# First expert layer of a two-layer mixture-of-experts network on one core: upward products a tile ahead of the downward ones, and two buffers for the result rows

## What is computed

```python
xf = _ln_t(t).reshape(-1, 256)                 # 4096 tokens
probs = softmax(xf @ gate_w.T)                 # 8 experts
vals, idx = top_k(probs, 2)
w = vals / (vals.sum(-1, keepdims=True) + 1e-08)
h = einsum('nd,ehd->neh', xf, w1)              # 512 hidden
g = einsum('nd,ehd->neh', xf, w3)
eo = einsum('neh,edh->ned', silu(h) * g, w2)
t = t + einsum('ned,ne->nd', eo, comb)         # comb holds w at idx
```

## Time and profile before

| what | value |
|---|---|
| device time, median of 3 runs | 1194.84 us (1193.18 to 1196.61) |
| profiled execution | 1198.09 us |
| its span in the profile | 1196.3 us |
| busy share of the span | PE 75%, DVE 64%, ACT 51%, POOL 43% |
| first expert layer, start of tile 0 on PE to start of tile 34 | 316.39 to 627.04 us |
| DMA engines' busy share, tiles 4 to 33 | 0.86 |
| granted TensorE clock, tiles 4 to 33 | 1.00 of full speed |

### The profile page before, as it was taken

The page is one execution under the profiler, slowest core; times in us unless marked ns, Lnnn a source line. Parts: engine busy times, 40 slices in busy tenths (PEclk is TensorE's granted clock), DMA queues, the critical chain, the costliest instruction groups (busy, mean ns, idle before and its releaser), DMA issues.

```text
span 1196.3 us, 25602 instructions
## 1 busy us (share of the span) xinstructions
PE 892.9 (75%) x7009; PEld 723.3 (60%) x7009; DVE 765.6 (64%) x1916; ACT 613.6 (51%) x1345; POOL 508.7 (43%) x408
## 2 busy tenths in 40 slices
PE   5320286855589999999994751579999999999975
PEld 4200165741367777777773640168888888888863
DVE  5899788999455555655653788835555555555540
ACT  4447286857365565565662245835434444444433
POOL 1288000000256666666663230045556555555540
PEclk8655598975699999999997875579999999999996
DMA  8249274990378888888887533255666465664438
GB/s 256 71 141 316 70 252 153 295 295 1 80 185 207 200 203 207 205 202 211 202 204 216 190 115 102 79 111 118 126 117 141 76 144 114 120 136 75 75 62 281
DMA packets 208566, 190.01 MB, mean 159 GB/s; under 512 B 98752, under 2 KB 184200, under 8 KB 208392
## 3 DMA queue, kind: packets, MB, share of 16 engines
q1 hardware_dynamic: 148344, 108.48, 32.2%
q0 software_dynamic: 27440, 38.97, 18.9%
q10 hardware_dynamic: 32736, 42.02, 11.4%
HBM read 111.22 MB, written 58.79 MB: 142 GB/s over the span
## 4 chain that ended last, share of the span: by engine, by line
PE 36%; DVE 19%; issue 15%; DMA 14%; ACTq 7%; ACT 7%; SPq 1%; DVEq 1%; POOL 0%; POOLq 0%
PE bank L796 15%; PE bank L774 13%; DMA wreg<-in_L_ffn_w_dram 5%; DMA rows_y<-region 4%; PE bank L838 2%; ACTq L313 2%; DVE region L1194 2%; DVE xt L1215 2%; ACT region L1065 2%; ACTq L1033 2%; ACT region L1069 2%; DVE region L1192 1%; PE bank L682 1%; DVE region L1583 1%; ACTq L314 1%
## 5 line engine op out<-in xcount | busy, mean ns | idle before, releaser
L774 PE MATMUL bank<-xt,wreg 128*128 x3360 | 385.1, 275 | 28.4 <-DMA xt<-region 25.7
L774 PEld LDWEIGHTS bank<-xt,wreg 128*128 128x128 f16 x3360 | 327.8, 99 | 79.9 <-issue 38.2
L542 POOL DMA_INDIRECT rows_y<-region x140 | 249.3, 1781 | 179.8 <-ACT region L1091 92.4
L796 PE MATMUL bank<-wreg,region 128*128 128x256 f16 x2520 | 294.5, 273 | 22.9 <-ACT region L1069 16.6
L796 PEld LDWEIGHTS bank<-wreg,region 128*128 128x128 f16 x2520 | 234.6, 98 | 77.5 <-ACT region L1069 30.6
L492 POOL DMA_INDIRECT region<-rows_x,region x148 | 151.6, 1024 | 270.6 <-DVE region L1492 153.5
L1074 ACT ACTIVATE region<-bank,b_t,wreg 128x256 f32<-128x256 f32 x280 | 136.0, 560 | 21.2 <-PE bank L774 20.2
L1091 ACT ACTIVATE region<-region 128x256 f32<-128x256 f32 x70 | 31.7, 500 | 193.6 <-DVE region L1598 183.0
L1065 ACT ACTIVATE region<-bank,fac 128x256 f32<-128x256 f32 x140 | 58.3, 465 | 97.7 <-PE bank L774 55.2
L1593 DVE SCALAR_TENSOR_TENSOR region<-region,wreg 128x512 f16<-128x512 f32 x140 | 105.1, 751 | 5.0
L1590 DVE TENSOR_SCALAR region<-region,wreg 128x512 f16<-128x512 f32 x140 | 70.0, 500 | 51.8 <-ACT region L1074 51.7
(11 more groups left out here) (273 smaller groups left out, 1120.3 us busy)
## 6 DMA issues: line engine op xcount, KB each, us to landing
wreg<-in_L_ffn_w_dram SPq DMA_DIRECT2D x80, 512.0 KB, 5.9
wreg<-in_L_ffn_w_dram ACTq DMA_DIRECT2D x72, 256.0 KB
split_v<-wreg ACTq DMA_DIRECT2D x36, 512.0 KB
wreg<-split_v SPq DMA_DIRECT2D x32, 512.0 KB
rows_x<-region SPq DMA_DIRECT2D x16, 512.0 KB, 5.1
rows_y<-tok SPq DMA_DIRECT2D x16, 512.0 KB, 6.1
tok<-rows_y SPq DMA_DIRECT2D x16, 512.0 KB, 6.0
wreg<-in_x_dram SPq DMA_DIRECT2D x4, 1024.0 KB, 9.5
```

What stands on the lines that cost most here:

```text
L542: nc.gpsimd.indirect_dma_start(rows_y[f], bass.IndirectOffsetOnAxis(ap=now[:, b, g_, 1:2], axis=0), y_rows[:, g_, :], None, compute_op=ALU ...
L774: last = pe.matmul(to, block, x_cols[:, bass.ds(b, 1), :, xs_, k, :].rearrange("p j r n -> p (j r) n"), start=(k == 0 and ws_ + xs_ == 0), ...
L796: last = pe.matmul(yb[:, r * C:(r + 1) * C], lhs[:, c, r * P:(r + 1) * P], block, start=first, stop=end, skip_group_check=True)
```

## The change

Only the first expert layer's order changes, and the places that depend on it.

- PE makes the upward products of tile n and then the downward products of tile n - 1 (`down0`). Ahead of tile 1 there is one set of downward products on unset data; after the loop there is one more set, of the last tile. The downward products' weights are addressed by a register (`of`, the expert of the tile in front). `up` waits for `hid_ready` of the tile in front before it writes a bank again.
- ACT does four SiLU, then the result of the tile in front (`result_of_last`), then the four copies of `hid`, then the piece as before. After the loop it copies the last result.
- DVE makes all four products and then the four subtractions. The products wait for the subtractions of the tile in front (`lo_ready`).
- The result rows have two buffers (`y_pair`), each with its own semaphore (`y_put`). POOL waits for the result one tile later: `y_copied` counts two more. It also waits, at the start of a tile, for the put of two tiles ago.
- `factors_y` has four buffers. Initial counts (`LAG`) let the first tile pass.

```diff
+        LAG = 4
+        y_pair = region[:, 1024:2048].rearrange("p (j g c) -> p j g c", j=2, g=2)
-        factors_y = region[:, 7880:7884].rearrange("p (j g) -> p j g", j=2)
+        factors_y = region[:, 7880:7888].rearrange("p (j g) -> p j g", j=4)
...
                     for g_ in range(2):
                         nc.gpsimd.indirect_dma_start(rows_y[f], bass.IndirectOffsetOnAxis(ap=now[:, b, g_, 1:2], axis=0),
-                                                     y_rows[:, g_, :], None, compute_op=ALU.add).then_inc(y_free[f], 16)
+                                                     (y_pair[:, b], y_rows)[f][:, g_, :], None, compute_op=ALU.add
+                                                     ).then_inc((y_put[b], y_free)[f], 16)
...
                         for r in range(2):
                             pool.wait_ge(xr_loaded[r][f], 16 * t + 48)
+                        if f == 0:
+                            pool.wait_ge(y_put[b], 32 * p + 16)
                         copy_lists(t, b)
...
-                        after(t, lambda m: pool.wait_ge(y_copied[f], m + 1))
+                        after(t, lambda m: pool.wait_ge(y_copied[f], m + 1 + later))
                         put(b)
...
-            def up(f, e, h, b):
-
-                ws = (w1_s, w3_s) if f == 0 else (v_s,)
+            def up(f, e, h, n):
+
+                ws, b = (w1_s, w3_s) if f == 0 else (v_s,), n % 2
                 for c in (2 * h, 2 * h + 1):
+                    if f == 0:
+                        pe.wait_ge(hid_ready, LAG * n + c + 1)
...
+            def down0(w2_of, tile):
+
+                pe.wait_ge(y_copied[0], tile + 1)
+                for c in range(4):
+                    pe.wait_ge(hi_ready[0], LAG * tile + c + 1)
+                    for hs in range(2):
+                        if hs == 1:
+                            pe.wait_ge(lo_ready[0], LAG * tile + c + 1)
...
-                            up(f, e, h, n % 2)
-
-                        for h in range(halves):
-                            down(f, e, n, h, halves)
+                            up(f, e, h, n)
+
+                        if f == 0:
+                            of = e - 1 + (n - edges[e] + 63) // 64 if e else e
+                            down0(lambda c, s_: w2_s[:, of, c, s_, :] if e == 0 else
+                                  w2_s[:, bass.ds(of, 1), c, s_, :].rearrange("p a n -> p (a n)"), n)
...
+                if f == 0:
+                    with pe.Fori(edges[E], edges[E] + 1) as n:
+                        down0(lambda c, s_: w2_s[:, E - 1, c, s_, :], n)
...
+            def result_of_last(n):
+
+                act.wait_ge(y_ready[0], n + 1)
+                before = n * 63 // 64
+                act.wait_ge(y_put[0], 32 * (before // 2) + 16)
+                act.wait_ge(y_put[1], 32 * (before * 63 // 64 // 2) + 16)
+                for g_ in range(2):
+                    last = act.activation(y_pair[:, bass.ds((n + 1) % 2, 1), g_, :].rearrange("p a c -> p (a c)"), yb[:, g_ * C:(g_ + 1) * C], ACT.Copy,
+                                          scale=factors_y[:, bass.ds((n + 3) % 4, 1), g_:g_ + 1].rearrange("p a b -> p (a b)"))
+                last.then_inc(y_copied[0], 1)
...
-                                for c in (2 * h, 2 * h + 1):
-                                    act.wait_ge(hid_ready, 2 * halves * n + c + 1)
-                                    act.activation(hid_hi[:, c], hid[:, h, (c % 2) * TILE:(c % 2 + 1) * TILE], ACT.Copy
-                                                   ).then_inc(hi_ready[f], 1)
...
                         if f == 0:
+                            result_of_last(n)
+                            for c in range(4):
+                                act.wait_ge(hid_ready, LAG * n + LAG + c + 1)
+                                act.activation(hid_hi[:, c], hid[:, c // 2, (c % 2) * TILE:(c % 2 + 1) * TILE], ACT.Copy
+                                               ).then_inc(hi_ready[f], 1)
                             split_hi(n)
...
+            with act.Fori(edges[E], edges[E] + 1) as m:
+                act.wait_ge(factors_y_ready, m)
+                result_of_last(m)
...
-                                    dve.wait_ge(silu_done[f], 2 * halves * n + c + 1)
+                                    dve.wait_ge(silu_done[f], LAG * n + c + 1)
+                                    dve.wait_ge(lo_ready[f], LAG * n + c + 1)
...
+                            for c in range(4):
+                                dve.wait_ge(hi_ready[f], LAG * n + LAG + c + 1)
+                                dve.tensor_tensor(hid_lo[:, c], half(hid[:, c // 2], c), hid_hi[:, c], ALU.subtract
+                                                  ).then_inc(lo_ready[f], 1)
```

More of the change, by code:

```diff
@@ L777, in up @@
                         last.then_inc(z_ready[f], 1)
-            def down(f, e, tile, h, halves):
+            def down0(w2_of, tile):
[5 more added lines that the diff above has]
+                            pe.wait_ge(lo_ready[0], LAG * tile + c + 1)
+                        lhs = (hid_hi, hid_lo)[hs][:, c]
+                        for r, ws_ in ((0, 0), (0, 1), (1, 0), (1, 1)) if hs == 0 else ((0, 0), (1, 0)):
+                            last = pe.matmul(yb[:, r * C:(r + 1) * C], lhs[:, r * P:(r + 1) * P], w2_of(c, ws_),
+                                             start=(c == 0 and r == 0 and hs + ws_ == 0), stop=(c == 3 and hs == 1),
+                                             skip_group_check=True)
+                last.then_inc(y_ready[0], 1)
```

82 lines of the change are left out of this document (44 added, 38 removed).

## The result

The changed kernel takes 1230.95 us (median of 4 runs, 1223.73 to 1238.87), the kernel before 1195.72 (4 runs): ratio 1.0297, 95% interval 1.0240 to 1.0353. It is slower by 35 us, where 1190.3 was forecast and 1206 was the top of the range. The profiled execution took 1236.06 us, its span is 1234.3.

A forecast was written before the change was run, and what follows sets the result against it. Links per tile were PE 8.3, ACT 8.4, POOL 8.4, fetch 8.5 us; 8.7 was taken against 8.99. Gains of 8.7 and 1.2 less 5.4 for the drain gave 4.5 us won, hence 1190.3 us, range 1178 to 1206.

The forecast's parts named there:

- The fetch link: POOL fetches tile n+3 only behind the put of tile n-1, now later; taken as the highest link, 8.5 us a tile.
- 3T = 15.2 + D: T is the tile time, 15.2 us from upward products to fetch, D from fetch through transposes; three tiles close the loop.
- its rival: Fetches and transposes slowed beside ACT's pieces: D 12.1 to 12.7, T 9.1 to 9.3, total 1202.3 to 1208 us; chance 0.22.
- I take 10.3: Choice for D, in us, between 9.1 measured with little DMA load and 18 at most; gives T = 8.5.
- the 15.2: Us from upward products' start to fetch: PE 8.2, result copies 0.9, on to the put 0.9, put to fetch 5.0.
- Queues in turn: DMA engines serve queues with work a packet at a time, so overlap with pieces doubles fetch and transpose time.
- A late piece should hold ACT less often: On ACT, the result copy between a piece's load and split lengthens first SiLU to split from 4.04 to 4.5 us.
- the surplus: Time per tile above the highest link, from links taking turns and single stalls: 0.46 us before, 0.25 taken after.
- the rivals at 8.9: ACT stays the bound with its surplus, T = 8.9: total 1196.3 us, up to 1199; chance 0.16.
- PE's turn: PE's own time per tile from upward and downward products: 8.2 to 8.6 us, taken 8.3.
- Drain: After the last tile, its put starts 16.6 us after the tile instead of 11.2: 5.4 us lost.
- 86% load: The DMA engines' busy share in the loop before, cited in favour of the slower fetch link case.

The follow-up runs named there:

- run 4: The changed kernel with each of ACT's two piece loads cut to 64 of 512 columns, stores whole: 1182.69 us, 0.9878 of the kernel before.
- run 3: The changed kernel with 12 filler matmuls per tile behind the downward products, into an unused bank: 1228.68 us, 1.0260 of the kernel before.
- run 6: The changed kernel with ACT's piece DMAs issued behind its four SiLU, after a wait for the piece under way: 1206.77 us, 1.0105 of the kernel before.
- Run 2: The changed kernel with POOL fetching the first layer's rows one tile further ahead (t+4 instead of t+3): 1217.54 us, 1.0181 of the kernel before.
- run 14: The changed kernel with piece DMAs issued by SP behind its transposes, rows fetched a tile further ahead, start mended: 1158.79 us, 0.9697 of the kernel before.
- run 13: The changed kernel with the three piece DMAs issued by SP behind its two transposes, and the start mended: 1219.63 us, 1.0171 of the kernel before.
- 15: The kernel before with the three piece DMAs issued by SP behind its transposes: 1184.26 us, 0.9901 of the kernel before.
- 5: The changed kernel with rows fetched a tile further ahead and ACT's piece DMAs behind its four SiLU, with a wait: 1205.64 us, 1.0097.
- 9: The changed kernel with rows fetched a tile further ahead, first count earlier, and ACT's piece DMAs ahead of the split, with a wait: 1237.75 us, 1.0373.
- 12: The kernel before with ACT's three piece DMAs, and a wait, between the two halves of a tile: 1291.61 us, 1.0800 of the kernel before.

## Why the prediction was wrong

**The fetch link.** 3T = 15.2 + D was the right equation, and its rival was the right mechanism, with too small a chance (0.22) and too small a price (1202 to 1208). The failed step is "I take 10.3" for D: it measured 12.9 in the mean of ten turns. I took it from fetches that land a microsecond later under load, and the earlier trace rows for the transposes, although no row showed them issued beside ACT's pieces. The fetches were about right (3.57 us); from the first fetch to the second transpose's issue it is 5.2 us, against 5.4 at the first tile of the kernel before; all the growth is in the landing of the transposes, 7.2 us for 3.4. With D = 12.9 and the 15.2 the tile would be 9.4. The rest, to 10.0, is in the 15.2, which measured 17.1: PE, held for 2.8 to 5.0 us, runs its next upward products at the lower clock in eight turns of ten, 1.5 us more in the mean, a feedback that the sum lacked, and 0.4 us is left. The runs bear out the two sizes: with small loads (run 4) the link is 15.5 + 9.9, close to what I had forecast. What mending the clock alone would give isn't shown (run 3).

**Queues in turn.** The rule quoted from the Trainium skill (DMA: Bandwidth & Descriptors, Queues, rings and completion order), that the engines serve queues with work in turn, stood in the prediction with its consequence that an overlap doubles the transposes' time. The runs agree with the doubling, though none shows the packets' turns: 3.6 us apart from the pieces (run 6), 7.2 beside them, 4.7 beside the whole store and an eighth of the loads (run 4). I gave it too little weight.

**ACT and the pieces.** "A late piece should hold ACT less often" failed: late pieces hold it 17.9 us in the loop, where it was 3.3. Run 2 takes the fetch link away and has 9.52 us, not 8.4 to 8.7, as the same meeting makes a piece land in 6.4 us instead of 4.2. So the surplus and the rivals at 8.9 were beside the point; the real second bound was not among them.

**PE and fill.** PE's turn, taken as 8.2 to 8.6, is 7.88: 5.24 us from upward to downward products and 2.64 on to the next tile, where I had 5.32 from a tile of the old order and 2.90 from its first. Tiles 0 to 3 won 3.0 us, where I forecast 1.2 and nothing for the fill. The start's 1.8 us was missed: I costed the initial counts at nothing and didn't look at what DVE does before it gives them.

**Drain.** Forecast 5.4 us, measured 4.7, and the closeness is partly luck. The last put starts 17.7 us after the tile, not 16.6, and 6.6 us later than before instead of 5.4; 1.7 us of it are the slow last upward products, which the sum didn't have. Behind the put 1.9 us come back (13.3 us on to the next stage, 15.2 before), which it didn't have either. In run 14 the end is 2.4 us shorter than in the change, but 1.7 of that are the clock; in run 13, with the issues gone from ACT too, it is 34.1 us. So the 2.2 us priced for ACT's DMA issues aren't shown.

**86% load.** I counted it for the fetch link, as if near a ceiling. Run 14 shows a share of 1.04, so that 1 isn't its ceiling, at 232 GB/s, against 0.86 and 204 before, and is the fastest. The load in itself was not the bound; when the transfers were issued was.

What stays open: why transfers lengthen in run 3, what the low clock costs by itself, whether the pieces' queue or their time of issue makes run 14 fast, and how much of run 14's gain over 15 the new order itself brings.

## What to carry to other kernels

A reordering that lets PE run ahead also delays whatever hangs on the last product of a tile: follow each loop through POOL, the DMA and SP back to PE over as many tiles as there are buffers, and price its transfers by what is issued in the same microsecond, not by their lone landing. A change that loses can be held by two links of which taking away either gives little (10.00 to 9.52 or 9.81 us a tile here, both 7.92), so test them together before you drop it. Keep bulk transfers that have a tile's time to land out of the microsecond of the small ones that somebody waits for; here they went behind these in the same queue.

## What the runs showed of the hardware

- The second of two transposes lands in 3.6 us in the mean apart from the pieces' issue (run 6, 24 on the chain), and in 6.4 to 8.0 when 1 MB of another queue is issued within a microsecond or so (the change, ten on the chain).
- Two waits, each in a loop of one turn, and three DMA issues keep ACT from its next operation for 2.7 to 2.9 us (the change); with a third such wait for 3.3 to 4.4 (runs 5, 9, 12).
- In the change, after 4.27 us without a matmul, 48 matmuls took 7.81 us at a granted clock of 0.68, and the next 48 5.40 us at 1.00.
- In run 14 the DMA engines carried 232 GB/s over 238 us at a busy share of 1.04, 14% above the 204 that they carry in the kernel before at 0.86.
